# Weights of the second batch's expert products addressed through a register instead of a fixed place

## The chip, the cores and the metric

One NeuronCore of a Trainium2 chip. The metric is the device time of one execution in microseconds (us), lower is better.

## The reference

Two sequences of 2048 tokens with 128 features (`x` is 2 x 2048 x 128) go through one transformer layer with adaptive normalisation. First an attention part, then a mixture of experts:

```
h = layernorm(x) * (1 + cb) + sb                       # per batch
scores = sigmoid(h @ router_w.T); 4 of 16 experts chosen, weights `combine`
h_e = h @ gate_w[e];  u_e = h @ up_w[e]                # 16 experts, 128 x 128 each
y_e = (silu(h_e) * u_e) @ down_w[e]
out = x + gb * (sum_e combine[e] * y_e  +  shared expert)
```

The shared expert is 256 wide and is treated as two more experts of 128, so that there are EX = 18 experts. Every expert is computed for every token, and an expert that wasn't chosen has weight zero. The numbers of the experts whose weights are multiplied are therefore known when the program is written: they run 0 to 17 for each chunk of tokens.

## The kernel before

The kernel is written engine by engine, with semaphores by hand. All engines follow one order of work (`run`): the attention of batch 0, then 144 expert steps `s` (2 batches x 4 chunks of 512 tokens x 18 experts). Beside the first 72 steps the attention of batch 1 is computed, cut into small pieces. The last 72 steps are the second batch's, and little else runs beside them: the routing of the last chunk on VectorE.

The steps of the two batches differ (`smooth(s)` is true for the first batch). The change touches only steps that are not smooth. In such a step TensorE's program is, in this order:

- `gate(s + 1)`: wait for `silu_ready`, which frees the PSUM bank, then one `pair` with the gate weights `wg`. A `pair` is three matmuls in float16 halves (lines 879, 880 and 881): high weights by high data, high weights by low data, low weights by high data. Here the weights are the stationary operand, 128 x 128, and 512 tokens are streamed.
- the down product of expert `d = s - 3`: wait for `act_split` and for `expert_added` (which frees one of two PSUM banks), then four `pair`s, one for each 128 tokens. Here the tokens (`gp`) are the stationary operand and the down weights (`wd_high`, `wd_low`) are streamed, 128 columns. The two halves of the shared expert are added up in one PSUM bank, so one step in 18 has no down product and the next has eight pairs.
- `up()`: wait for `act_ready`, then one `pair` with the up weights `wu`.

ScalarE computes silu of the gate product (line 830). VectorE multiplies it with the up product (line 1753). ScalarE makes the high half of it (line 847) and GpSimd the low half (line 635); `act_split` tells of that. After its product VectorE adds the down product of expert `s - 3` to `x`, in four instructions of 128 columns that carry each token's weight (line 1736), and then raises `expert_added`. Each engine executes its program in order. A wait stands in its engine's program ahead of the instruction that it guards, either as an instruction of its own (EVENT_SEMAPHORE) or as a part of that instruction.

`expert_added` is awaited at line 1216 and `act_split` at line 1207. The matrices of all 18 experts are in SBUF by then: `wg` and `wu` are tiles of 128 x 2 x 18 x 128 float16, and `wd_high` and `wd_low` are views of 128 x 18 x 128.

Of the kernel before, what the change touches and what calls it, by code (L numbers as in the profile page):

```python
# [22 lines left out]
P = 128  # L23
# [3 lines left out]
W = 512  # L27
CH = N // W
PER = W // P
E = 16  # L30
NS = 2
EX = E + NS
# [114 lines left out]
def build(nc, hs, Wq, bq, Wk, bk, Wv, bv, Wo, bo, Wtq, btq, Wfq, bfq, router_w, router_b,  # L147
# [3 lines left out]
    with ctx:  # L151
        def sb(name, shape, dt=F32):
            return ctx.enter_context(nc.sbuf_tensor(name, shape, dt))

        def sem(name):
            return ctx.enter_context(nc.semaphore(name))
# [23 lines left out]
        wg = sb("wg", [P, 2, EX, P], F16); wu = sb("wu", [P, 2, EX, P], F16); wd = sb("wd", [P, EX, P])  # L180
# [11 lines left out]
        h2 = sb("h2", [P, 2, N], F16)  # L192
# [11 lines left out]
        wd_high, wd_low = (row[:, k, 0:EX * P // 2].bitcast(F16).rearrange("p (e d) -> p e d", e=EX) for k in (1, 2))  # L204
# [29 lines left out]
        tri = sb("tri", [P, GRP, GRP])  # L234
        grank = sb("grank", [P, BLK, GRP]); gsel = sb("gsel", [P, BLK, GRP])
        best = sb("best", [P, BLK, 8]); bidx = sb("bidx", [P, BLK, 8], U32); bf = sb("bf", [P, BLK, 8])
        iota = sb("iota", [P, E]); iotai = sb("iotai", [P, E], mybir.dt.int32)
        wsum = sb("wsum", [P, BLK]); comb = sb("comb", [P, BLK, E])
        combT = sb("combT", [E, 2, W])

# [44 lines left out]
        gate_made = sem("gate_made"); up_made = sem("up_made"); down_made = sem("down_made")  # L285
# [53 lines left out]
        def gate_bank(s):  # L339
            return bank[((3, 5) if smooth(s) else (3, 2))[s % 2]]  # L340

        def up_bank(s):
            return bank[4 if smooth(s) else (4, 5)[s % 2]]

        def adds_before(d):

            n = d - (NB - 1) * STEPS
            return ADDS * (n // EX) + min(n % EX, E)

        def down_bank(s):  # L350
            return bank[6 if smooth(s) else adds_before(s) % 2]
# [40 lines left out]
        def smooth(s):  # L392


            return s < (NB - 1) * STEPS

        def ends_chunk(s, lag):

            return s >= lag and (s - lag) % EX == EX - 1
# [69 lines left out]
        def _(pool):  # L469
            chain = Chain(pool, pool_step)  # L470
# [3 lines left out]
                                          base=0, pattern=[[-1, P]], channel_multiplier=1)); chain.settle()  # L474
# [11 lines left out]
            chain.step(pool.memset(minus[:, :], 0.0))  # L486
            chain.step(pool.memset(identb[:, :], 0.0))
            chain.step(pool.iota(iotai[:, :], pattern=[[1, E]], base=0, channel_multiplier=0))
            w_den = float(N) * N - 1
            for n, wgt in enumerate((4.0, 8.0, 4.0, -2.0, 2.0 * N)):  # L490
                chain.step(pool.memset(vw[:, n:n + 1], wgt / w_den))
# [2 lines left out]
                                          base=0, pattern=[[-1, P]], channel_multiplier=1))  # L494
            chain.step(pool.affine_select(out=minus[:, :], in_=minus[:, :], compare_op=ALU.not_equal, fill=-HUGER,
                                          base=0, pattern=[[-1, P]], channel_multiplier=1))

            chain.step(pool.affine_select(out=causal[:, :], in_=causal[:, :], compare_op=ALU.is_ge, fill=1.0,
                                          base=0, pattern=[[-1, P]], channel_multiplier=1))
            chain.step(pool.affine_select(out=tri[:, :, :], in_=tri[:, :, :], compare_op=ALU.is_ge, fill=1.0,  # L500
                                          base=0, pattern=[[-1, GRP], [1, GRP]], channel_multiplier=0))
            chain.step(pool.memset(selx[0:3, :], HUGE))
            chain.step(pool.affine_select(out=sely[:, :], in_=sely[:, :], compare_op=ALU.is_ge, fill=0.0,
                                          base=-(FEAT - 3), pattern=[[0, P]], channel_multiplier=1))
# [356 lines left out]
        def _(pe):  # L861
# [15 lines left out]
            def pair(out_bank, weights, data, start=True, stop=True):  # L877

                mm(out_bank, weights[0], data[0], start=start, stop=False)  # L879
                mm(out_bank, weights[0], data[1], start=False, stop=False)  # L880
                return mm(out_bank, weights[1], data[0], start=False, stop=stop)  # L881
# [246 lines left out]
            def turn_weights(c, dst):  # L1128

                for k in range(PER):  # L1130
                    last = pe.transpose(dst[0:E, k * P:(k + 1) * P], comb[:, c * PER + k, :], ident[:, :])
                last.then_inc(comb_turned, 1)

            def late(b, t):
# [6 lines left out]
                if t == LATE_STEPS - 1 and b == 0:  # L1141
                    pe.wait_ge(comb_ready, 2)
                    turn_weights(CH - 1, bank[7])

            def step(s):
                b, e, c = s // STEPS, s % EX, s // EX % CH
                data = [h2[:, h, c * W:(c + 1) * W] for h in range(2)]
                if s == 0:

                    pe.wait_ge(scores_masked, NCH)  # L1150
                    pe.wait_ge(turned_copied, NCH)
                    pe.wait_ge(row_ready, BLK)
                    pe.wait_ge(stage_used, 4)
                    pe.wait_ge(wd_loaded, 32)
                def gate(s):
                    e, c = s % EX, s // EX % CH
                    if e == 0 and c in (0, CH - 1):
                        pe.wait_ge(mix_split, CH * (s // STEPS) + (CH if c else CH - 1))
                    if s == (NB - 1) * STEPS + 1:

                        pe.wait_ge(turned_copied, NB * NCH)
                    elif s >= 2 and smooth(s - 2):

                        pe.wait_ge(hidden_ready, s - 1)
                    elif s >= 2:

                        pe.wait_ge(silu_ready, s - 1)
                    pair(gate_bank(s)[:, :], [wg[:, h, e, :] for h in range(2)],
                         [h2[:, h, c * W:(c + 1) * W] for h in range(2)]).then_inc(gate_made, 1)

                if s == 0:
                    gate(0)
                if s + 1 < NB * STEPS:
                    gate(s + 1)
                def up():
                    if s and smooth(s - 1):

                        pe.wait_ge(act_ready, s)
                    elif s and smooth(s - 2):

                        pe.wait_ge(hidden_ready, s - 1)
                    elif s:
                        pe.wait_ge(act_ready, s - 1)
                    pair(up_bank(s)[:, :], [wu[:, h, e, :] for h in range(2)], data).then_inc(up_made, 1)

                if ends_chunk(s, 3) and smooth(s - 3):

                    f = (s - 3) // EX
                    pe.wait_ge(y_copied, f + 1)
                    for k in range(PER):  # L1190
                        last = pe.transpose(bank[6][:, k * P:(k + 1) * P], ysb[:, k * P:(k + 1) * P], ident[:, :])
                    last.then_inc(y_turned, 1)
                    if s < NB * STEPS:
                        up()
                if s >= 2 and smooth(s - 2):
                    d = s - 2
                    pe.wait_ge(act_ready, d + 1)
                    if d % EX == 0 and d:

                        pe.wait_ge(out_ready, d // EX)  # L1200
                    mm(bank[6][:, :], wd[:, d % EX, :], act_g[:, d % 2, :], start=(d % EX == 0),  # L1201
                       stop=(d % EX == EX - 1)).then_inc(down_made, 1)
                if not smooth(s - 3):

                    d = s - 3
                    n = d - (NB - 1) * STEPS
                    pe.wait_ge(act_split, n + 1)
                    if n == 0:

                        pe.wait_ge(wd_ready, DOWN_PIECES)  # L1210
                        pe.wait_ge(scores_masked, NB * NCH)
                        pe.wait_ge(dist_used, NB * NCH)
                    if d % EX != E:
                        if adds_before(d) >= 2:

                            pe.wait_ge(expert_added, adds_before(d) - 1)
                        both = (d - 1, d) if d % EX > E else (d,)
                        for k in range(PER):
                            for at in both:
                                last = pair(down_bank(d)[:, k * P:(k + 1) * P],  # L1220
                                            [gp[:, (at - (NB - 1) * STEPS) % HELD, h, k * P:(k + 1) * P] for h in range(2)],
                                            [half_of[:, at % EX, :] for half_of in (wd_high, wd_low)],
                                            start=at == both[0], stop=at == d)
                        last.then_inc(down_made, len(both))
                if s < NB * STEPS and not (ends_chunk(s, 3) and smooth(s - 3)):
                    up()

            run(first, inputs, attention, step, late)

        @block.vector  # L1230
# [550 lines left out]
```

## Time and profile before

| | |
|---|---|
| median of 2 runs | 628.36 us (628.35 and 628.36) |
| the profiled execution | 626.02 us |
| its span, first to last instruction | 624.3 us |
| outside the span | 1.7 us |
| granted TensorE clock, mean | 0.976 |
| TensorE matmuls busy | 556.8 us, 89% |
| VectorE, ScalarE, GpSimd busy | 490.7, 363.7, 353.4 us |

The profile describes one execution, 2.3 us shorter than the median. PE is the array's matmuls, PEld the weight loads, which run beside them. The duration of a matmul in the rows is longer than the distance from one matmul to the next, since they are pipelined: the rate is read from the starts. Instructions that only the engine's sequencer executes (waits, register moves, DMA issues) are marked with a q and are not counted as busy.

### The profile page before, as it was taken

The page shows a single profiled execution, that of the slowest core. Times are in us where ns is not written, and L with a number is a line of the kernel's source. Part 1 is how long each engine was busy: PE and PEld are TensorE (multiplying, and loading weights), DVE is VectorE, ACT ScalarE, POOL GpSimd, SP SyncE. Part 2 cuts the span into 40 slices and gives each one's busy share as a digit, 9 for nine tenths or more (in the row PEclk, how much of TensorE's full clock was granted, in tenths as well). Part 3 has the DMA queues.
Part 4 walks back from the last instruction along what each step waited for, and adds up shares of the span by engine and source line. Part 5 has one row for each costly group of instructions (what it writes and reads, how often), then busy time and mean ns, then how long its engine had stood idle before and what let it go on. Part 6 is the DMA issues. An engine that isn't in the chain of part 4 may idle for free. (4 is left out here: it accounts for less than half of the span.)

```text
span 624.3 us, 10923 instructions
## 1 busy us (share of the span) xinstructions
PE 556.8 (89%) x3508; PEld 334.7 (54%) x3508; DVE 490.7 (79%) x1428; ACT 363.7 (58%) x729; POOL 353.4 (57%) x339
## 2 busy tenths in 40 slices
PE   6898778978767998989989999899798999999996
PEld 5655445556534543545545555555455565656664
DVE  6869999987867896459667667558986999989886
ACT  5267657885436334546866776674447555545552
POOL 7678659351035518497876696453215555555553
PEclk9989999989879999989999999999999999999998
DMA  8500100000042212312012121121100000000000
GB/s 220 147 2 2 38 1 1 2 1 2 5 120 68 74 64 68 84 53 85 17 56 94 39 69 34 51 85 53 34 1 17 3 13 7 2 19 1 18 2 18
DMA packets 23425, 26.02 MB, mean 42 GB/s; under 512 B 2676, under 2 KB 13960, under 8 KB 23368
## 3 DMA queue, kind: packets, MB, share of 16 engines
q1 hardware_dynamic: 22928, 24.80, 13.6%
q8 instruction: 28, 0.46, 0.3%
q10 hardware_dynamic: 440, 0.53, 0.3%
q14 instruction: 29, 0.24, 0.1%
HBM read 23.09 MB, written 2.23 MB: 41 GB/s over the span
## 5 line engine op out<-in xcount | busy, mean ns | idle before, releaser
L621 POOL TENSOR_TENSOR sw<-hid,gp 128x512 f32<-128x512 f32 x64 | 81.4, 1271 | 80.4 <-DVE hid L1690 75.2
L635 POOL TENSOR_TENSOR gp<-stage,gp 128x512 f16<-128x512 f32 x72 | 83.8, 1164 | 65.5 <-ACT gp L847 65.5
L1690 DVE SCALAR_TENSOR_TENSOR hid<-stage,bank 128x512 f32<-128x512 f32 x72 | 49.3, 685 | 56.4 <-ACT stage L830 55.8
L830 ACT ACTIVATE stage<-bank 128x512 f32<-128x512 f32 x144 | 84.6, 589 | 15.1 <-PE bank L881 14.7
L571 POOL TENSOR_TENSOR row<-row,dx 128x512 f32<-128x512 f32 (+3 forms) x48 | 55.7, 1160 | 51.1 <-ACT dx L686 50.5
L782 ACT COPY ptr<-bank 128x512 f32<-128x512 f32 (+2 forms) x80 | 41.4, 518 | 70.4 <-PE bank L1082 69.3
L847 ACT CAST gp<-stage 128x512 f16<-128x512 f32 x72 | 44.4, 617 | 64.6 <-DVE stage L1753 64.6
L1100 PE MATMUL bank<-v,ptr 128*128 128x128 f32 x544 | 76.3, 281 | 4.6 <-DVE x L1508 4.6
L1201 PE MATMUL bank<-stage,wd 128*128 128x512 f32 x144 | 75.3, 605 | 5.0 <-DVE x L1697 5.0
L1100 PEld LDWEIGHTS bank<-v,ptr 128*128 128x128 f32 x544 | 69.6, 197 | 7.2 <-issue 5.8
L1736 DVE SCALAR_TENSOR_TENSOR x<-bank,comb,x 128x128 f32<-128x128 f32 x256 | 71.5, 342 | 0.1
L879 PE MATMUL bank<-h,wu 128*128 128x512 f16 x144 | 55.2, 383 | 7.3 <-DVE stage L1716 7.0
L1753 DVE SCALAR_TENSOR_TENSOR stage<-bank,stage 128x512 f32<-128x512 f32 x72 | 49.6, 689 | 14.7 <-ACT stage L830 8.0
L788 ACT ACTIVATE row<-row,nmx 128x512 f32<-128x512 f32 (+2 forms) x80 | 52.8, 659 | 13.5 <-DVE nmx L1538 13.5
L1716 DVE TENSOR_TENSOR stage<-bank,sw 128x512 f32<-128x512 f32 x64 | 44.0, 687 | 18.7 <-POOL sw L621 12.0
L879 PE MATMUL bank<-row,gp 128*128 128x128 f16 x288 | 52.6, 221 | 6.7 <-DVE x L1736 5.1
L879 PE MATMUL bank<-h,wg 128*128 128x512 f16 x144 | 55.3, 384 | 0.2
L881 PE MATMUL bank<-h,wg 128*128 128x512 f16 x144 | 55.4, 385 | 0.0
L880 PE MATMUL bank<-h,wg 128*128 128x512 f16 x144 | 55.4, 384 | 0.0
L880 PE MATMUL bank<-h,wu 128*128 128x512 f16 x144 | 55.0, 382 | 0.0
L881 PE MATMUL bank<-h,wu 128*128 128x512 f16 x144 | 54.9, 381 | 0.0
L1082 PE MATMUL bank<-ident,row 128*128 128x128 f32 x272 | 45.0, 282 | 9.4 <-ACT row L788 5.1
(251 smaller groups left out, 1270.3 us busy)
## 6 DMA issues: line engine op xcount, KB each, us to landing
gp<-shares SPq DMA_DIRECT2D x64, 256.0 KB, 3.2
out_x<-x SPq DMA_DIRECT2D x8, 256.0 KB, 2.3
x<-in_L_attn_hidden_states SPq DMA_DIRECT2D x4, 256.0 KB, 5.3
stage<-in_L_ffn_gate_w SPq DMA_DIRECT2D x1, 576.0 KB, 5.0
stage<-in_L_ffn_up_w SPq DMA_DIRECT2D x1, 576.0 KB, 4.2
stage<-in_L_ffn_gate_w SPq DMA_DIRECT2D x1, 448.0 KB, 5.5
stage<-in_L_ffn_up_w SPq DMA_DIRECT2D x1, 448.0 KB, 3.4
row<-in_L_wmod ACTq DMA_DIRECT2D x1, 384.0 KB
```

The lines of the kernel that those rows point to most:

```text
L571: pool.tensor_tensor(o, o, dx[:, pooled(b, m) % 2, 0:w], ALU.subtract).then_inc(measure_ready, 1)
L621: pool.tensor_tensor(sw[:, s % 2, :], hid[:, s % 2, :], wb[:, n % HELD_WEIGHTS, :], ALU.mult)\
L635: pool.tensor_tensor(gp[:, n % HELD, 1, :], act_g[:, s % 2, :], gp[:, n % HELD, 0, :], ALU.subtract)\
L788: act.activation(row[:, i % ROWS, lot], row[:, i % ROWS, lot], ACT.Exp, bias=nmx[:, i:i + 1], accum_out=rsum[:, i, c:c + 1]).then_inc(prob ...
L830: act.activation(sg[:, s % 2, :], gate_bank(s)[:, :], func, scale=half_of / (H_UP * W_UP))\
L879: mm(out_bank, weights[0], data[0], start=start, stop=False)
L880: mm(out_bank, weights[0], data[1], start=False, stop=False)
L881: return mm(out_bank, weights[1], data[0], start=False, stop=stop)
L1100: last = mm(ring(b, 3, i)[:, 0:P], ptr[:, m % 2, k * P:(k + 1) * P], v[:, j, :], start=(j == 0), stop=(j == i))
L1201: mm(bank[6][:, :], wd[:, d % EX, :], act_g[:, d % 2, :], start=(d % EX == 0), stop=(d % EX == EX - 1)).then_inc(down_made, 1)
L1736: last = dve.scalar_tensor_tensor(out=own, in0=y, scalar=weight, in1=own, op0=ALU.mult, op1=ALU.add)
L1753: dve.scalar_tensor_tensor(out=act_g[:, s % 2, :], in0=up_bank(s)[:, :], scalar=G_UP / (H_UP * W_UP), in1=sg[:, s % 2, :], op0=ALU.mult, o ...
```

## The change

A row of 18 integers, `expert`, is written once at the start by GpSimd (values 0 to 17). In the second batch's steps TensorE's sequencer reads the number of the expert from this row into a register before each gate product, each up product and each expert's down product, and the address of the weights is the tile's base plus that number times the size of one matrix. The number is the one that the program had as a constant before. The matmuls, their order, their data and the waits stay. The first batch's steps keep constant addresses.

```
+iota(expert[:, :], pattern=[[1, EX]], base=0, channel_multiplier=0)      # once, on GpSimd

+def of_expert(s, weights):
+    if smooth(s):
+        return [weights[:, h, s % EX, :] for h in range(2)]
+    e = pe.value_load(expert[0:1, s % EX:s % EX + 1], min_val=0, max_val=EX - 1)
+    return [weights[:, h, bass.ds(e, 1), :].rearrange("p o d -> p (o d)") for h in range(2)]
...
-pair(gate_bank(s)[:, :], [wg[:, h, e, :] for h in range(2)], ...)
+pair(gate_bank(s)[:, :], of_expert(s, wg), ...)
...
-pair(up_bank(s)[:, :], [wu[:, h, e, :] for h in range(2)], data)
+pair(up_bank(s)[:, :], of_expert(s, wu), data)
...
+held = {at: pe.value_load(expert[0:1, at % EX:at % EX + 1], min_val=0, max_val=EX - 1) for at in both}
 for k in range(PER):
     for at in both:
         last = pair(down_bank(d)[:, k * P:(k + 1) * P],
                     [gp[:, (at - (NB - 1) * STEPS) % HELD, h, k * P:(k + 1) * P] for h in range(2)],
-                    [half_of[:, at % EX, :] for half_of in (wd_high, wd_low)],
+                    [half_of[:, bass.ds(held[at], 1), :].rearrange("p o d -> p (o d)")
+                     for half_of in (wd_high, wd_low)],
```

There are 72 loads for gate products, 72 for up products and 72 for down products, 216 in all.

## Rows read from the trace of the kernel before

**Rows 1.** The page: span, and busy time of each engine.
```profile
span 624.3 us, 10923 instructions
PE 556.8 (89%) x3508; PEld 334.7 (54%) x3508; DVE 490.7 (79%) x1428; ACT 363.7 (58%) x729; POOL 353.4 (57%) x339
```

**Rows 2.** Stretches: length, busy time and count of each engine, granted clock, DMA.
```profile
462.80:476.20 13.40, 11.74 (x71) 5.63 (x69) 9.16 (x20) 9.46 (x19) 4.74 (x5) 1.00 0.07 20
476.20:618.00 141.80, 135.23 (x1233) 84.92 (x1231) 127.80 (x380) 75.98 (x137) 80.30 (x70) 1.00 0.03 7
618.40:624.30 5.90, 2.23 (x23) 1.96 (x19) 0.90 (x5) 0.00 (x0) 0.00 (x0) 0.50 0.15 44
```

**Rows 3.** TensorE's groups by line and form, 476.2 to 618 us.
```profile
L879 PE MATMUL bank<-row,gp 128*128 128x128 f16 x276 | 49.6, 219 | 5.1 <-DVE x L1736 5.1
...
L879 PE MATMUL bank<-h,wu 128*128 128x512 f16 x68 | 25.8, 379 | 0.0
...
L879 PE MATMUL bank<-h,wg 128*128 128x512 f16 x67 | 25.4, 379 | 0.0
```

**Rows 4.** Timeline of TensorE's matmuls in one step: start, duration.
```profile
605.71 0.38 PE L879 MATMUL bank<-h,wg 128*128 128x512 f16 x1
...
606.36 0.22 PE L879 MATMUL bank<-row,gp 128*128 128x128 f16 x1
...
606.97 0.22 PE L881 MATMUL bank<-row,gp 128*128 128x128 f16 x1
607.03 0.38 PE L879 MATMUL bank<-h,wu 128*128 128x512 f16 x1
...
607.68 0.38 PE L879 MATMUL bank<-h,wg 128*128 128x512 f16 x1
```

**Rows 5.** Timeline of VectorE in the same stretch.
```profile
604.62 1.12 DVE L1736 SCALAR_TENSOR_TENSOR x<-bank,comb,x 128x128 f32<-128x128 f32 x4
605.97 0.69 DVE L1753 SCALAR_TENSOR_TENSOR stage<-bank,stage 128x512 f32<-128x512 f32 x1 [0.24 <-ACT stage L830]
```

**Rows 6.** Timeline of GpSimd in the same stretch.
```profile
603.46 1.16 POOL L635 TENSOR_TENSOR gp<-stage,gp 128x512 f16<-128x512 f32 x1 [0.80 <-ACT gp L847]
```

**Rows 7.** Chain that ended last, at one of VectorE's late steps.
```profile
519.76 1.04 DVE x L1736 x4
520.80 0.14 issue
520.94 0.22 PE bank L879
```

**Rows 8.** Timeline of TensorE's weight loads behind that wait.
```profile
520.94 0.10 PEld L880 LDWEIGHTS bank<-row,gp 128*128 128x128 f16 x1
...
521.55 0.10 PEld L879 LDWEIGHTS bank<-h,wu 128*128 128x128 f16 x1
```

**Rows 9.** Instructions of the sequencers at three lines: count, duration min/median/max ns.
```profile
L1216 PEldq EVENT_SEMAPHORE  x66: 51/51/851, 477.3 to 617.2; - x66
...
L421 SPq MOVE_SHAPE wd<-in_L_ffn_down_w x1: 368/368/368, 12.3 to 12.3; - x1
...
L495 POOLq MOVE  x1: 29/29/29, 3.9 to 3.9; - x1
```

**Rows 10.** The page's DMA issues: KB each, us from issue to landing.
```profile
out_x<-x SPq DMA_DIRECT2D x8, 256.0 KB, 2.3
```

**Rows 11.** Timeline of TensorE at the end of the span.
```profile
618.14 0.22 PE L879 MATMUL bank<-row,gp 128*128 128x128 f16 x1 [1.60 <-POOL gp L635]
...
619.14 0.32 PE L879 MATMUL bank<-row,gp 128*128 128x128 f16 x1
...
620.00 0.32 PE L881 MATMUL bank<-row,gp 128*128 128x128 f16 x1
```

**Rows 12.** Timeline of GpSimd at the start.
```profile
3.51 0.13 POOL L488 IOTA iotai<- 128x16 int32 x1
```

More of the change, by code:

```diff
@@ L236, in build @@
         best = sb("best", [P, BLK, 8]); bidx = sb("bidx", [P, BLK, 8], U32); bf = sb("bf", [P, BLK, 8])
-        iota = sb("iota", [P, E]); iotai = sb("iotai", [P, E], mybir.dt.int32)
+        iota = sb("iota", [P, E]); iotai = sb("iotai", [P, E], mybir.dt.int32); expert = sb("expert", [1, EX], mybir.dt.int32)
         wsum = sb("wsum", [P, BLK]); comb = sb("comb", [P, BLK, E])
@@ L488, in _ @@
             chain.step(pool.iota(iotai[:, :], pattern=[[1, E]], base=0, channel_multiplier=0))
+            chain.step(pool.iota(expert[:, :], pattern=[[1, EX]], base=0, channel_multiplier=0))
             w_den = float(N) * N - 1
@@ L1167, in gate @@
                         pe.wait_ge(silu_ready, s - 1)
-                    pair(gate_bank(s)[:, :], [wg[:, h, e, :] for h in range(2)],
-                         [h2[:, h, c * W:(c + 1) * W] for h in range(2)]).then_inc(gate_made, 1)
+                    pair(gate_bank(s)[:, :], of_expert(s, wg), [h2[:, h, c * W:(c + 1) * W] for h in range(2)])\
+                        .then_inc(gate_made, 1)
                 if s == 0:
@@ L1183, in up @@
                         pe.wait_ge(act_ready, s - 1)
-                    pair(up_bank(s)[:, :], [wu[:, h, e, :] for h in range(2)], data).then_inc(up_made, 1)
+                    pair(up_bank(s)[:, :], of_expert(s, wu), data).then_inc(up_made, 1)
                 if ends_chunk(s, 3) and smooth(s - 3):
```

## The prediction

> **What bounds the kernel now.** I read the page's busy times first: the array (PE) is busy 89% of a span of 624.3 us [rows 1]. An average over the kernel says little about the place that is changed, so the stretches come next. From 476.2 to 618 us, where only second-batch steps run, PE is busy 135.23 of 141.80 us at full granted clock, and VectorE 127.80 us [rows 2]. TensorE's groups give the idle time of that stretch: 5.1 us in all, each time until VectorE's add to `x` had freed a PSUM bank [rows 3]. The other 136.7 us are matmuls back to back. The timeline of one step shows the pace: gate products from 605.71, down products from 606.36, up products from 607.03, the next gate at 607.68 [rows 4]. That is 1.97 us a step: 1.30 for six matmuls of 512 columns (0.216 each) and 0.67 for twelve of 128 columns (0.0557 each). The array sets the period, and whatever adds array time or starves the array is paid at once.
>
> **What the sequencer does now.** Each matmul is two instructions, a weight load and the matmul, so a step has 36. The change leaves the array's work alone and adds to TensorE's sequencer, so its spare time decides. No row shows the sequencer's time for a matmul directly. An upper bound comes from a place where it had nothing queued: an add ends at 520.80, the first matmul starts 0.14 us later [rows 7], and from 520.94 to 521.55 eleven more weight loads start and as many matmuls with them, 22 instructions in 0.61 us [rows 8]. So at most 28 ns each, 36 x 0.028 = 1.0 us a step, and 0.05 us for the wait at line 1216 [rows 9]. Of each 1.97 us it has 0.9 us to spare.
>
> It can't spend that freely. Ahead of the down products it stands at `expert_added`. In the step shown, the add before ends at 604.62 + 1.12 = 605.74 and the down products start at 606.36 [rows 4, 5]. The gate products, already queued, cover 0.62 us, 0.14 of which the start itself takes. About half a microsecond can go in between unseen. `act_split` is no issue: its subtraction for an earlier expert ended at 603.46 + 1.16 = 604.62 [rows 6]. The waits for `silu_ready` and `act_ready` guard results of two steps before.
>
> **The change part by part.** The row of numbers: one iota on GpSimd at the start, 0.13 us as the one beside it [rows 12], 0.1 us against work that isn't waited for. Zero; if its cover were gone, 0.1 us.
>
> The loads: three a step. No register load from SBUF is in the trace. From below it is bounded by the cheapest thing that this sequencer executes itself, a wait, 0.051 us; from above by a whole transfer, issue to landing, 2.3 us [rows 9, 10]. I take 0.37 us, the duration of the longest plain sequencer instruction, a MOVE_SHAPE on SyncE [rows 9]: a read of one word must go out and come back, which is more than a wait costs, and much less than 256 KB, two transports and a completion. Three: 1.11 us. The Trainium skill (Runtime: NRT & Kernel Launch, "Instruction fetch mechanics") gives about 200 ns for each register of a load from HBM; no row here shows one. By that figure, as an estimate, three would be 0.6 us and the total below some 34 us less.
>
> The addresses: each load serves two places (high and low weights), each a multiplication and an addition, and `min_val`, `max_val` may be checked by two more instructions. Between none (folded into the instruction) and six, at 0.051 us each, since a wait is the only one of this sequencer's own instructions in the rows; a register move on GpSimd takes 0.029 [rows 9]. I take six, because nothing shows that they are folded: 0.31 us a load, 0.92 a step.
>
> The instructions that hold a register: the weight loads of gate and up (6) and the matmuls of down (12), 18 of 36. Between 28 ns, as before, and 28 + 51 = 79 if the sequencer needs another instruction's time to put the address in. I take 51: 18 x 0.051 = 0.92, the other 18 x 0.028 = 0.50. The Trainium skill (TensorE: Matmul & The Clock Gate, "Wait — 56ns, not 53.3ns?") gives 62 ns for a matmul that the sequencer's own program decodes. The rows with constant addresses speak against that for the kernel before (28 ns at most); if the register forces it, this term would be 1.1 us, as an estimate, and the total 13 us more.
>
> Nothing is removed. The waits change place: those ahead of a load now hold the sequencer instead of an instruction in TensorE's queue, and behind them stand the load and all 12 or 3 pairs. For gate and up they have long been fulfilled. For the down products it makes the chain add, load, addresses, first matmul.
>
> The sum for a step: 1.11 + 0.92 + 0.92 + 0.50 + 0.05 = 3.50 us of sequencer time, against 1.97 us of array time. The sequencer becomes the bound; the array idles 1.5 us a step, waiting for issue, and the 0.9 us to spare are already used in that figure. The stretch holds 67 gate products, 68 up products and 276 / 4 = 69 down products [rows 3], so 67 steps: 67 x 3.50 = 234.5 against 141.8, +92.7 us. The 5.1 us of waits for VectorE are inside the 141.8: at 3.5 us a step its 127.80 / 67 = 1.9 us fit, so they vanish. Before 476.2 lie 5 steps in 13.4 us [rows 2], on a chain through normalisation, with some 10 loads; I put 0.4 us of each on the path, +4. Behind 618 us lie the last down products, a load or two, +0.5. Together +97 us: 626.0 + 97 = 723 for the profiled execution, and as the median stands 2.3 us above it, 725.
>
> **The rivals.**
>
> *The load isn't overlapped.* If a load waits until the queued matmuls are done, or its answer takes as long as a transfer's, three times a step the array stands for load, addresses and restart: 1.97 + 3 x (0.37 + 0.31 + 0.14) = 4.43 us, 67 x 4.43 - 141.8 = +155 and the same 4.5 outside, 788 us. With 1.2 us for a load (half a transfer) in my sum the step is 3.50 + 3 x 0.83 = 6.0, 893 us. For it: nothing shows a load that runs beside the queue. Against: the wait of line 1216 does run beside queued gate products [rows 4, 5].
>
> *The clock falls.* After an idle time of 1.60 us at 616.5 to 618.14 the matmuls of 128 columns go from 0.056 apart to (620.00 - 619.14) / 8 = 0.107 [rows 11], and the granted clock of the rest is 0.50 [rows 2], the 1.2 GHz level. An array idle 44% of the time in pieces of 0.3 to 0.7 us could get there. Then its work is 1.97 x 0.107 / 0.0557 = 3.8 us a step, a bit over 3.5: +113 and 4.5, 746 us, perhaps 765 with the remaining gaps. Against: the pieces are shorter than that 1.6 us, and at the lower clock the array would be busy nearly all the time.
>
> *The other side: it is hidden.* The sequencer has 0.9 us a step to spare and 0.48 us behind the add. If load and addresses together cost under 0.3 us and instructions with registers no more than others, the period stays 1.97. Only the nine steps with a late VectorE [rows 3] and the early ones pay, (9 + 10) x 0.3 = 6 us: 632 to 634, not slower by 2%. It decides at 0.3 us a load. For it: a wait costs 0.051. Against: two bounds of three would both have to be near their floor. Cheap but not free (0.37 a load, nothing else) gives 1.11 + 1.0 + 0.05 = 2.16 us a step, +2.9 for the stretch and 4.5 outside: 636. A period of 2.3 us gives 645.
>
> *It does nothing.* The constants could be recovered ahead of the run, as the row is known, and 628 stays. Nothing in the code does that, since the number is read from memory.
>
> **How the numbers follow.** Sequencer-bound as summed, anywhere from 2.3 to 4.2 us a step (645 to 772): 0.60. Loads not overlapped or far dearer: 0.20. Clock: 0.09. Hidden: 0.10. Nothing: 0.01. The range reaches from 645 (2.3 us a step) to 880 (near the dear load); below lie the hidden cases and above the dearest, some 0.18 together. 2% is 12.6 us, about what a measurement of this kernel can tell from no change. Slower by more than that: 0.89; within: 0.10; faster: 0.01, since no part removes work or lets a transfer start earlier.
>
> **What would show it.** In the stretch of second-batch steps: PE's busy share near 60% with an unchanged count; gaps ended by issue, not by VectorE; register loads in TensorE's sequencer at 0.37 us, 216 of them; gates 3.5 us apart; the twelve down matmuls 0.08 us apart or more instead of 0.056; VectorE's, ScalarE's and GpSimd's own durations unchanged, the first 462 us unchanged. If the clock's rival holds, the granted clock falls to 0.5 there. I am wrong if the down matmuls stay at 0.056 and gates at 1.97, or if the gaps sit in front of each load and have its whole length beyond the queued work. The weakest terms are the load and the six address instructions.

## The result and the profile after

The changed kernel takes 685.99 us (median of 2 runs, 684.15 and 687.82) against 628.36: ratio 1.092, 95% interval 1.079 to 1.104. The forecast was 725, between 645 and 880. The profiled execution took 684.15 us with a span of 682.4, 58.1 more than the span of before [rows 1]. The unchanged first batch takes a little longer or shorter in each execution: the second batch's first gate product is at 461.5 us here, at 462.8 before, and at 464.5 to 470.0 in the runs below. So small differences are read from the distances within the batch and not from totals.

The page after, span and busy time of each engine:

```profile
span 682.4 us, 12004 instructions
PE 592.9 (87%) x3508; PEld 326.3 (48%) x3508; DVE 492.2 (72%) x1428; ACT 364.4 (53%) x729; POOL 353.7 (52%) x340
```

The matmuls are the same 3508, and VectorE, ScalarE and GpSimd are busy for the same time within 2 us; what is new is 1081 instructions, 1080 of them on TensorE's sequencer. PE seems busier by 36 us with the same work. That is how a matmul's duration is drawn: it is longer than the distance to the next one (0.38 us drawn, 0.216 apart), so in a tight row the durations overlap and are counted once, and with a pause behind it the whole duration counts. The share of busy time therefore hides short pauses; starts don't.

The stretches after (length, busy time and count of PE, PEld, DVE, ACT, POOL, then granted clock, DMA):

```profile
462.80:476.20 13.40, 11.89 (x67) 4.89 (x66) 7.85 (x18) 9.64 (x18) 5.04 (x5) 1.00 0.07 21
476.20:676.00 199.80, 171.62 (x1232) 77.47 (x1230) 129.72 (x381) 76.01 (x136) 79.89 (x69) 1.00 0.02 5
```

The second row holds the work of the 141.80 us of before, 1232 matmuls against 1233 [rows 2], and takes 58.0 us more, all of the difference. The clock is 1.00, the 2.4 GHz level, in both.

What TensorE waited for in that stretch, as the groups have it (after the bar: idle time before, and what ended it):

```profile
L880 PE MATMUL bank<-row,gp 128*128 x276 | 53.8, 221 | 17.5 <-issue 16.6 <-POOL gp L636 0.7
...
L880 PE MATMUL bank<-h,wu 128*128 128x512 f16 x68 | 26.3, 387 | 3.0 <-issue 1.0
...
L880 PE MATMUL bank<-h,wg 128*128 128x512 f16 x66 | 25.6, 387 | 6.2 <-issue 1.8
```

The 5.1 us of waits for VectorE's add [rows 3] are gone. Of the 26.7 us of idle time 19.4 are put down to "issue" and 0.7 to GpSimd; the rest is in pauses too short to be given a cause. "Issue" means that no semaphore released the matmul: its own sequencer was late. One step of the timeline shows where:

```profile
600.35 0.38 PE L882 MATMUL bank<-h,wu 128*128 128x512 f16 x1
600.90 0.39 PE L880 MATMUL bank<-h,wg 128*128 128x512 f16 x1 [0.17 <-issue]
...
601.34 0.38 PE L882 MATMUL bank<-h,wg 128*128 128x512 f16 x1
601.92 0.23 PE L880 MATMUL bank<-row,gp 128*128 x1 [0.20 <-issue]
602.04 0.23 PE L881 MATMUL bank<-row,gp 128*128 x1
602.11 0.22 PE L882 MATMUL bank<-row,gp 128*128 x1
602.16 0.22 PE L880 MATMUL bank<-row,gp 128*128 x1
...
602.61 0.22 PE L882 MATMUL bank<-row,gp 128*128 x1
602.84 0.39 PE L880 MATMUL bank<-h,wu 128*128 128x512 f16 x1
```

From 600.35 to 600.90 are 0.55 us where [rows 4] have 0.216; from 601.34 to 601.92 0.58; from 602.61 to 602.84 0.23 where 0.056 would do. Those are the three loads. Within the down products the pace is the old 0.056, except behind the first matmul (0.12). Over the last 66 distances between gate products the median is 2.90 us, before 1.965; the means are 2.914 and 2.054 and differ by 0.860 x 66 = 56.8 us.

The sequencer's new instructions and its wait for `expert_added`, from the views of four lines (count, min/median/max ns):

```profile
L1150 PEldq TENSOR_LOAD <-expert x144: 294/302/492, 460.1 to 671.3; - x144
L1150 PEldq FUSED_REGOPS  x144: 151/151/165, 460.7 to 671.7; - x144
L1150 PEldq SEQ_ASSERT  x144: 18/18/24, 460.9 to 671.9; - x144
...
L1226 PEldq TENSOR_LOAD <-expert x72: 294/300/415, 472.9 to 676.3; - x72
...
L880 PEldq FUSED_REGOPS  x216: 46/46/65, 461.0 to 677.2; - x108
...
L1224 PEldq EVENT_SEMAPHORE  x66: 51/51/855, 478.5 to 674.7; - x66
```

For each of 216 numbers: the load, 0.30 us; a long register instruction and an assertion, which are the check of `min_val` and `max_val`; and two short register instructions, one for each address (the second stands at line 882 or 881).

What these cost the sequencer is the distance of their starts, not their duration. In this trace, as medians over the last 66 steps: from a load to its check 0.361 us, from the check to the first address 0.286, from that to the second address 0.124 (down 0.138), from there to what comes next 0.124 (down 0.149), and 0.106 from the wait to the load behind it. Three times 0.647, and 0.386, 0.397 and 0.106, are 2.83 us a step. Besides, 70 of these distances are longer than their median by 0.03 to 0.16 us, which makes 0.08 us a step; no run shows why. Together that is the mean period of 2.91 with hardly anything left over: the sequencer does not stand still. The wait for `expert_added` never held it within those steps (0.051 us each time; the 0.855 lies behind the last gate product).

### The profile page after: what moved, and what is told of

Read it like the earlier page. It is cut to its first block and busy times, and to the rows that moved or that the text cites. A ratio compares the mean times of both kernels' runs of the same rounds, so it can differ in the third digit from the quotient of the medians.

```text
span 682.4 us, 12004 instructions
## 1 busy us (share of the span) xinstructions
PE 592.9 (87%) x3508; PEld 326.3 (48%) x3508; DVE 492.2 (72%) x1428; ACT 364.4 (53%) x729; POOL 353.7 (52%) x340
## 5 line engine op out<-in xcount | busy, mean ns | idle before, releaser
L880 PE MATMUL bank<-row,gp 128*128 x288 | 56.1, 221 | 20.4 <-issue 19.6
L880 PEld LDWEIGHTS bank<-row,gp 128*128 128x128 f16 x288 | 28.0, 97 | 53.4 <-issue 53.3
```

## The experiments

Theory A: the sequencer executes one thing after the other, its times add up to 2.90 us a step, and only what exceeds the array's 1.97 us, or stands behind a wait that ends late, costs anything. The sum of starts above already says so for the change. Its rivals are B, each load stops the array for its whole length; C, instructions with a register are slow themselves; D, the waits that moved from a queued instruction to the sequencer are what costs. All periods below are the median of the last 66 distances between gate products in the trace.

**e4: the up product twice.** Three more matmuls of 512 columns a step.

```
 own = of_expert(s, wu)
+if not smooth(s):
+    pair(up_bank(s)[:, :], own, data)
 pair(up_bank(s)[:, :], own, data).then_inc(up_made, 1)
```

> The changed kernel with each second-batch up product computed twice into the same bank (three more matmuls of 512 columns a step, 0.65 us of array time, array 2.61 us a step; the result is the same). Theory A: the sequencer's 2.87 us a step still is more than the array's 2.61, so the added array time disappears in the gaps: 686 to 692 us. Theory B (array and loads take turns): 68 x 0.65 = 44 us more, 730 us.

Measured: 692.15 us, ratio 1.101 (1.094 to 1.108), against 1.092 (1.079 to 1.104) of the change, so no difference within the intervals; in the profiled executions 4.9 us of it lie ahead of the second batch (466.4 us against 461.5). The period is 2.905 us against 2.899. The timeline:

```profile
600.09 0.39 PE L880 MATMUL bank<-h,wu 128*128 128x512 f16 x1 [0.17 <-issue]
...
600.74 0.38 PE L880 MATMUL bank<-h,wu 128*128 128x512 f16 x1
...
601.39 0.38 PE L880 MATMUL bank<-h,wg 128*128 128x512 f16 x1
...
602.20 0.23 PE L880 MATMUL bank<-row,gp 128*128 x1
...
603.12 0.39 PE L880 MATMUL bank<-h,wu 128*128 128x512 f16 x1
```

The gate product follows the second up product without a pause (0.65 from 600.74 to 601.39): its load was made meanwhile. 44 us of array time went into the gaps, and B is out. The six added instructions also show what a matmul or weight load costs the sequencer: (2.905 - 2.899) / 6, some 1 ns, as far as a difference of two medians can tell. The change's own trace agrees: behind a down product's second address stand 22 of them, behind a gate product's two, and the next instruction comes 0.149 against 0.124 us later, 1.2 ns for each. In e2 24 of them take 0.084 us between the wait and the next load, 3.5 ns each. So a few ns at most.

**e6: the loads ahead of the waits.** Each `value_load` is moved in front of the waits of its product (the cut shows the gate product's).

```
+own = of_expert(s, wg)
 ... pe.wait_ge(silu_ready, s - 1)
-pair(gate_bank(s)[:, :], of_expert(s, wg), ...)
+pair(gate_bank(s)[:, :], own, ...)
```

> The changed kernel with each register load ahead of the waits of its product instead of behind them. Theory A (the sum of the sequencer's time decides, the waits have been fulfilled): the same, 684 to 688 us. Theory D (the waits that now hold the sequencer are what costs): clearly less, under 670 us.

Measured: 687.08 us, ratio 1.089 (1.083 to 1.095), period 2.897. The place of a load doesn't matter while the sequencer is the bound, and D is out for the change.

**e8: every load twice**, with its check, the first one unused.

```
+pe.value_load(expert[0:1, s % EX:s % EX + 1], min_val=0, max_val=EX - 1)
 e = pe.value_load(expert[0:1, s % EX:s % EX + 1], min_val=0, max_val=EX - 1)
```

> The changed kernel with every load, and its range check, made twice. Theory A: 3 x 0.66 = 1.97 us more of sequencer time, with nothing to hide in: 2.87 + 1.97 = 4.84 us a step, 67 x 1.97 = 132 us more, 818 us, a few more for the early steps. Theory C: no change in the matmuls, hence a smaller gain of time than 60 us.

Measured: 828.9 us, ratio 1.315 (1.308 to 1.322), period 4.877. One load with its check costs (4.877 - 2.899) / 3 = 0.66 us of the sequencer. The view of the row `expert` has 432 loads, unchanged in length (these are the 288 for gate and up products):

```profile
L1150 PEldq TENSOR_LOAD <-expert x144: 293/300/492, 467.6 to 817.2; - x144
L1151 PEldq TENSOR_LOAD <-expert x144: 293/300/716, 468.5 to 817.9; - x144
```

**e5: no range check.**

```
-pe.value_load(expert[0:1, at % EX:at % EX + 1], min_val=0, max_val=EX - 1)
+nc.values_load(expert[0:1, at % EX:at % EX + 1], engines=[PE], min_val=0, max_val=EX - 1,
+               skip_runtime_bounds_check_because="the row holds 0 to 17")
```

> The changed kernel with the loads' range check left out (FUSED_REGOPS of 151 ns and SEQ_ASSERT of 18 ns behind each load, with the pauses around them 0.29 us of the 0.75). Theory A: 2.87 - 3 x 0.29 = 2.0 us a step, 0.03 above the array: about 58 us less than the change, 628 to 638 us. Theory B (the load's round trip of 0.30 us is what hurts): 686 less a third at most, over 665 us.

Measured: 639.46 us, ratio 1.018 (1.010 to 1.026), period 2.033. The check takes (2.899 - 2.033) / 3 = 0.29 us, though its two instructions last 0.169; the rest are pauses between the sequencer's instructions. The load then is 0.66 - 0.29 = 0.37 us, 0.30 and its pause. The trace of the change gives the same by the starts, 0.286 and 0.361. 46.5 of the 57.6 us hang on the check alone, because without it the sum is nearly the array's 1.97.

**e3: registers, but hardly a load.** Eight loads in all; the expert's number is added to a register.

```
+def number(s):
+    if s // EX not in bases:
+        bases[s // EX] = [pe.value_load(expert[0:1, n:n + 1], min_val=0, max_val=1) for n in range(2)]
+    e = s % EX
+    return bases[s // EX][0] + e if e < EX - 1 else bases[s // EX][1] + (EX - 2)
```

> All places of second-batch weights still come from a register, but the registers are loaded twice a chunk (8 loads instead of 216) and the number of the expert is added to them. Theory A: six address instructions a step at about 0.12 us with their pauses are 0.75 us of sequencer time, under the array's 1.97: 628 to 632 us. Theory C (register-addressed weight loads and matmuls themselves are slow): well above 640 us.

Measured: 631.15 us, ratio 1.002 (0.999 to 1.005), period 1.965.

```profile
L1151 PEldq TENSOR_LOAD <-expert x8: 298/303/483, 465.2 to 582.9; - x8
```

All 18 register-addressed instructions of a step and the six address computations are there (two of the six are a shorter instruction, 32 ns, that adds the number), and nothing is to be measured. C is out.

**e2 and e1: one half of the change each.** In e2 the down products have constant places again, in e1 the gate and up products.

```
 e2: -held = {at: pe.value_load(...) for at in both}
     -[half_of[:, bass.ds(held[at], 1), :]...     +[half_of[:, at % EX, :] ...
 e1:  def of_expert(s, weights):
     +    return [weights[:, h, s % EX, :] for h in range(2)]
```

> Only gate and up products take their weights through a register. Theory A: sequencer 0.90 for up, 1.0 for gate with the wait, little for the down instructions: 1.95 us, as much as the array's 1.97, so nearly hidden but without any lead: 632 to 645 us. Theory B: 135 loads x 0.75 = 101 us more, less what the queue covers, over 686 us. Theory C: one third of the 58 us, 648 us.

> Only the down products take their weights through a register; gate and up products have constant places again. Theory A (the sequencer's own time adds up, and only what exceeds the array's 1.97 us a step, or stands behind the wait for expert_added, costs anything): the sequencer needs about 1.1 us a step, so the array sets the period; behind the add 0.76 us from load to first down product stand against 0.62 us of queued gate products, a gap of 0.1 to 0.3 us in some steps: 638 to 650 us. Theory B (each load stops the array for its whole length of 0.75 us): 69 x 0.75 = 52 us more than before, 680 us. Theory C (the cost lies in register-addressed matmuls, of which down has twelve and gate and up six): two thirds of the 58 us, 667 us.

Measured: e2 635.63 us, ratio 1.011 (1.002 to 1.020), period 1.989; e1 645.38 us, ratio 1.027 (1.021 to 1.034), period 2.142. The halves cost 7 and 16 us and together 58: what the sequencer can hide is there once, not once for each half. That one load a step costs more than two speaks for a place, not for an amount. e1's timeline of TensorE:

```profile
610.70 0.38 PE L882 MATMUL bank<-h,wg 128*128 128x512 f16 x1
611.01 0.23 PE L880 MATMUL bank<-row,gp 128*128 x1
611.16 0.23 PE L881 MATMUL bank<-row,gp 128*128 x1
611.22 0.22 PE L882 MATMUL bank<-row,gp 128*128 x1
```

And VectorE's add of the same step:

```profile
608.98 1.12 DVE L1743 SCALAR_TENSOR_TENSOR x<-bank,comb,x 128x128 f32<-128x128 f32 x4
```

The add ends at 608.98 + 1.12 = 610.10 and the first down product starts 0.91 us later, at 611.01. The array is through with the gate products at 610.70 + 0.22 = 610.92, so they cover 0.82 of it and 0.09 us are lost. The second address is computed only when the first matmul has been issued: 0.15 from 611.01 to 611.16 instead of 0.056, 0.09 more. Together 0.18, as much as 2.142 - 1.965.

**e11: e1 with the load ahead of the waits.**

```
+held = {at: pe.value_load(...) for at in both}
 pe.wait_ge(act_split, n + 1)
 ...
 pe.wait_ge(expert_added, adds_before(d) - 1)
-held = {at: pe.value_load(...) for at in both}
```

> Only the down products use a register, as in e1, but the load stands ahead of the waits for act_split and expert_added instead of behind them. If e1's 16 us come from the chain add, load, check, addresses, first down product, then with 0.5 us of these 0.76 taken out of it the 0.62 us of queued gate products cover the rest: 629 to 634 us. If they come from the load's time as such, wherever it stands: 645 us as e1.

Measured: 632.74 us, ratio 1.008 (1.004 to 1.012), period 1.965.

```profile
601.67 0.38 PE L882 MATMUL bank<-h,wg 128*128 128x512 f16 x1
601.89 0.22 PE L880 MATMUL bank<-row,gp 128*128 x1
601.94 0.22 PE L881 MATMUL bank<-row,gp 128*128 x1
```

Both gaps are gone, so it was the chain behind the add. The same move that was worth nothing in e6 is worth 13 us here, where the sequencer has time to spare.

**e7 and e10: one load for an expert**, its register kept for all three products; e10 without the check besides.

```
+if s not in number:
+    number[s] = pe.value_load(expert[0:1, s % EX:s % EX + 1], min_val=0, max_val=EX - 1)
+e = number[s]
```

> One load for an expert, its register kept for the gate, up and down products of that expert (72 loads). Theory A: 1.0 us for gate with load and wait, 0.3 each for the addresses of up and down: 1.6 to 1.7 us of sequencer time a step, under 1.97: 628 to 634 us. Theory B: 72 x 0.75 less what the queue covers, 645 to 680 us.

> One load for an expert, kept for its three products, and no range check. Of 1.97 us a step the sequencer uses about 1.3: 628 to 632 us, level with the kernel before. Not faster than it in any theory, since the array's work is the same.

Measured: e7 632.98 us, ratio 1.008 (1.004 to 1.011); e10 626.76 us, ratio 1.002 (0.998 to 1.006). The period is 1.965 in both. In total e7 is still some 3 us slower, its interval lies above 1; e10, with 626.76 us against 628.31 of the kernel before run beside it, can't be told from it. Register addressing can be had for nothing here, with one load and no check; no version is shown to be faster than the kernel before.

**e9: two numbers in each load**, each checked, the second unused.

```
-pe.value_load(expert[0:1, e:e + 1], ...)
+nc.values_load_multi_w_load_instructions(expert[0:1, e:e + 2], engines=[PE], min_val=0, max_val=EX - 1)[1][0]
```

> The changed kernel with two numbers (this expert's and the next place of the row) fetched by each load, each with its range check; the second isn't used. If both come in one trip, TENSOR_LOAD stays near 0.30 us and only the second check (0.29 us with its pauses) is added: 3.77 us a step, 686 + 67 x 0.87 = 744 us. If each register costs a trip of 0.2 us of its own, 0.6 us a step more: 784 us.

Measured: 802.47 us, ratio 1.280 (1.269 to 1.291), period 4.521. The line's view:

```profile
L1151 PEldq TENSOR_LOAD <-expert x144: 529/537/728, 465.6 to 789.0; - x144
```

The second number adds 0.235 us to the load, so the second register is fetched for nearly as much again and not along with the first, and another 0.29 for its check: 3 x 0.525 = 1.58 of the 1.62 us that the period grew. Both figures that I gave were too low. The first took the second number for free. The second, 784 us, had its check in it and took 0.2 us for the number: 0.6 + 0.87 = 1.47 us a step where 1.62 were measured. That makes 10 of the 18 us it missed by; the rest lies outside the stretch, 5.6 us of it ahead of the batch in the profiled executions.

## Why the prediction was right

**What bounds the kernel.** As read: the array before, the sequencer after, with "issue" behind nearly all of the idle time that has a cause, VectorE's waits gone and the clock at 1.00. The forecast case, 2.3 to 4.2 us a step, was the one that came; the period is 2.90 where the sum said 3.50.

**The terms.** The direction and the mechanism held; the sizes were off in both directions, and that they nearly cancelled is luck (below).
- The load: 0.37 taken, 0.30 measured, and 0.37 with the pause behind it (e5, e8). Right in size, but by luck: it was taken from a MOVE_SHAPE of another engine, which shows nothing of a load. The Trainium skill's 200 ns for each register (Runtime: NRT & Kernel Launch, "Instruction fetch mechanics") is stated for HBM; here, from SBUF, the second register costs 0.235 us (e9), which is near it, and the first 0.30, which is half as much again.
- Addresses and check: 0.31 a load taken. The check alone is 0.29 (e5). The rest of the period, (2.90 - 3 x 0.66) = 0.92 us a step, is two addresses a product, the wait ahead of the down products and their pauses, 0.31 a product. So 0.29 + 0.31 = 0.60 a load instead of 0.31: the term should have been twice as large, and it came out small because I counted instructions and not the pauses between them. In the rows of before a wait lasts 0.051 us [rows 9]; that its successor starts later than its end was not looked at. After the change the load behind such a wait starts 0.106 us from the wait's start.
- Instructions with a register: 0.92 taken, nothing measured (e3). The Trainium skill's 62 ns for a matmul decoded by the sequencer's program (TensorE: Matmul & The Clock Gate, "Wait — 56ns, not 53.3ns?") isn't seen either: 18 of them cost nothing (e3). The page gives that figure for matmuls with hardware decode off; no run here shows that setting.
- The other instructions: 0.50 taken from a bound of 28 ns each; e4 gives about 1 ns. This is the step that failed most. The 22 instructions in 0.61 us [rows 8] ran at the array's own pace of 0.056 us for a pair, so the row could only bound the sequencer from above, and the prediction used the bound as the value. The sum that holds is the one of the starts above, 2.83 + 0.08, with these 36 instructions inside it at some 0.05.

The two terms for instructions were together 1.4 us a step too high (0.92 + 0.50 against about 0.05), the one for addresses, check and wait about 0.8 too low (0.97 against 3 x 0.60 = 1.8). What is left, 3.50 - 2.90 = 0.60 us a step, makes 40 us over the 67 steps; forecast and result lie 39 apart. Two errors of opposite sign hide in that. Had only the instruction terms been put right, the sum would have been 1.11 + 0.92 + 0.05 + 0.05 = 2.13 us a step, which the prediction's own way of adding turns into 634 us: within 2%, and the wrong answer. It is the address and check term, too low as well, that kept the verdict. The spare time of the sequencer was about 1.8 us a step, not 0.9; this is why two loads a step nearly vanish (e2).

**Outside the stretch.** +4 for the early steps, measured +0.9: from the first gate product of the batch to the sixth it is 14.15 us (461.51 to 475.66) instead of 13.26 (462.76 to 476.02). +0.5 for the end, measured 1.8: from the last gate product to the end of the span 14.5 us instead of 12.7. With the 56.8 of the stretch that is 59.5; the 1.3 us by which the batch began earlier make it the 58.1 of the spans, within rounding.

**The chain behind the add.** The prediction named it (0.62 us of queued gate products as cover) and then dropped it, since the sum of the sequencer's time exceeds it. e6 bears that out for the change; e1 and e11 show it as the bound once the sum is small, with 0.76 us against the cover. That a load in a wait's shadow may cost more than two elsewhere wasn't foreseen.

**The rivals.** Not overlapped, 788: refuted by e4. Clock: it stayed at 1.00 with the array idle a third of the time, by starts, in pieces of 0.17 to 0.37 us. With more idle time it isn't out of reach: in e8 it fell now and then (last section). Hidden, 632 to 634, from which I said it decides at 0.3 us a load with its addresses: a load with check and addresses takes 0.90 us and three of them were too much, but one load for an expert, with three pairs of addresses, leaves the period at 1.965 (e7), since the budget was larger. Of the marks to look for, the loads were 216 but 0.30 us, the gates 2.90 apart and not 3.5, and two more were wrong: the down matmuls stay 0.056 apart but for the first, and PE's busy share is 86%, not 60%; by starts it is 1.965 / 2.90 = 68%.

## What to carry to other kernels

Ask of a register-addressed operand what its number costs, not what the instruction costs: a load from SBUF 0.37 us and a range check 0.29 us of the issuing sequencer, two addresses 0.2 to 0.3, the instructions themselves nothing. Keep the register for every use of the same number, leave the check out where the range is certain, and put the load ahead of a wait that ends late. And compare the sum with the time that the array's queued work gives to the sequencer: up to there it is free, beyond it each 0.1 us a step is paid in full (e8, e9).

## What the runs showed that I had not expected

A matmul or weight load costs TensorE's sequencer about 1 ns in e4 and in the change's trace, a hundredth of the 124 ns from one register instruction to the next. The range check costs nearly as much as the load (0.29 and 0.37 us). Two numbers in one load cost 0.235 us more than one, so a wide load saves about 0.13 us for each number against loads of their own.

In e8 the granted clock falls for a short time, with the array's work spread thin (1.97 us of it in 4.88):

```profile
702.43 0.61 PE L880 MATMUL bank<-h,wu 128*128 128x512 f16 x1
702.83 0.63 PE L881 MATMUL bank<-h,wu 128*128 128x512 f16 x1
703.25 0.63 PE L882 MATMUL bank<-h,wu 128*128 128x512 f16 x1
704.05 0.49 PE L880 MATMUL bank<-h,wg 128*128 128x512 f16 x1 [0.17 <-issue]
```

The stretch that holds these matmuls and the next one (columns as in the stretches above, the granted clock third from the end):

```profile
690.00:705.00 15.00, 9.09 (x55) 3.97 (x54) 6.02 (x18) 3.20 (x6) 3.46 (x3) 0.89 0.01 1
705.00:720.00 15.00, 7.65 (x54) 3.40 (x54) 6.28 (x21) 4.50 (x8) 4.09 (x4) 1.00 0.00 0
```

The matmuls of 512 columns are 0.42 apart at the 1.2 GHz level instead of 0.216, and at 704.38 they are fast again. In nine of the last 67 steps the up product's matmuls are that far apart. Mostly it costs nothing, since the sequencer sets the period; one distance between gate products among them is 5.35 us instead of 4.9. The next stretch shows 1.00 again, with the array's work spread just as thin.
